# Graph layer on one core: the next batch's preparation spread over three tiles, the last bank of picks reduced by VectorE, and a new order of work on ScalarE

## What is computed

```python
mask = A != 0                                  # A: 8 x 1024 x 1024
vals, idx = top_k(where(mask, -arange(N), -inf), 25)   # the first 25 neighbours of a row
agg = max over those neighbours of X[idx]      # X: 8 x 1024 x 128
agg = where(degree <= 25, maximum(agg, 0), agg)
out = relu(concat([X, agg]) @ W + b)
x = layernorm(X + out)
```

## Time and profile before

| | us |
|---|---|
| median of 3 runs (lowest, highest) | 750.28 (745.78, 757.25) |
| the profiled execution | 752.01 |
| its span in the trace | 750.3 |

### The profile page before, as it was taken

The page is one execution under the profiler, slowest core; times in us unless marked ns, Lnnn a source line. Parts: engine busy times, 40 slices in busy tenths (PEclk is TensorE's granted clock), DMA queues, the critical chain, the costliest instruction groups (busy, mean ns, idle before and its releaser), DMA issues.

```text
span 750.3 us, 13181 instructions
## 1 busy us (share of the span) xinstructions
PE 560.5 (75%) x3836; PEld 321.3 (43%) x3888; DVE 631.5 (84%) x948; ACT 483.2 (64%) x911; POOL 263.3 (35%) x318
## 2 busy tenths in 40 slices
PE   3767876877779677788868777788876977777772
PEld 2444443544335344354435444445443544444331
DVE  5888799977998789889998867989998879987794
ACT  6735675558855578557974757747895569643554
POOL 2525413353034431336313442044513444054400
PEclk9699999999989889799999988999999999999996
DMA  7611220313024120233204312043202411020102
GB/s 240 204 33 63 65 86 16 134 58 109 3 74 141 55 95 11 74 132 92 76 9 130 121 51 72 2 137 116 88 35 75 141 59 44 2 58 26 37 1 58
DMA packets 32682, 56.68 MB, mean 76 GB/s; under 512 B 4515, under 2 KB 21158, under 8 KB 32550
## 3 DMA queue, kind: packets, MB, share of 16 engines
q1 hardware_dynamic: 26150, 42.08, 16.6%
q0 software_dynamic: 6400, 13.12, 6.3%
HBM read 50.99 MB, written 4.19 MB: 74 GB/s over the span
## 4 chain that ended last, share of the span: by engine, by line
PE 29%; DVE 26%; issue 18%; ACT 9%; DVEq 8%; another core or an unknown queue 6%; DMA 4%; SPq 0%; ACTq 0%; POOL 0%; POOLq 0%
PE pair L977 20%; DVE part L714 9%; DVE agg_t L814 5%; DMA adj_sb<-in_adj 4%; DVE hot L708 4%; DVEq L786 2%; PE half L977 2%; DVE g_val L756 2%; ACT maskT L511 2%; DVE g_feat L785 2%; DVEq L826 1%; PE misc L1037 1%; ACT row_work L642 1%; PE p_maskT L949 1%
## 5 line engine op out<-in xcount | busy, mean ns | idle before, releaser
L977 PE MATMUL pair<-hot,x_part 128*128 128x512 bf16 (+2 forms) x1608 | 390.8, 382 | 86.9 <-DVE part L714 49.9
L714 DVE TENSOR_REDUCE part<-pair 128x128 f32<-128x1024 f32 x256 | 311.1, 1218 | 91.0 <-PE pair L977 68.9
L977 PEld LDWEIGHTS pair<-hot,x_part 128*128 128x128 bf16 x1608 | 146.5, 101 | 246.1 <-issue 76.6
L406 POOL DMA_INDIRECT g_feat<-in_x,g_idx x200 | 191.7, 959 | 121.8 <-issue 89.7
L443 POOL TENSOR_TENSOR y_sb<-relu_sb,x_sb 128x128 f32<-128x128 f32 x64 | 30.6, 478 | 342.5 <-ACT relu_sb L570 342.4
L814 DVE TENSOR_REDUCE agg_t<-part 128x128 f32<-128x1024 f32 (+2 forms) x56 | 113.6, 2028 | 0.2 <-ACT part L577 0.2
L511 ACT ACTIVATE maskT<-p_maskT 128x1024 bf16<-128x1024 bf16 x56 | 57.0, 1018 | 60.5 <-PE p_maskT L949 26.9
L708 DVE TENSOR_SCALAR hot<-V 128x1024 bf16<-128x1024 bf16 x224 | 84.5, 390 | 0.0
L577 ACT ACTIVATE part<-half 128x512 f32<-128x512 f32 x56 | 33.4, 597 | 69.6 <-PE half L977 51.2
L502 ACT ACTIVATE mask<-adj_sb 128x1024 bf16<-128x1024 int32 x56 | 58.9, 1053 | 26.3 <-DMA adj_sb<-in_adj 22.8
L518 ACT ACTIVATE V<-p_V 128x512 bf16<-128x512 f32 x98 | 58.3, 595 | 9.5 <-issue 5.0
(11 more groups left out here) (93 smaller groups left out, 590.0 us busy)
## 6 DMA issues: line engine op xcount, KB each, us to landing
adj_sb<-in_adj SPq DMA_DIRECT2D x56, 512.0 KB
g_adj<-in_adj SPq DMA_DIRECT2D x8, 512.0 KB, 4.1
x_sb<-in_x SPq DMA_DIRECT2D x8, 512.0 KB
out<-y_sb SPq DMA_DIRECT2D x7, 512.0 KB
g_feat<-in_x,g_idx POOLq DMA_INDIRECT x200
out<-y_sb SPq DMA_DIRECT2D x1, 448.0 KB
w_sb<-in_W SPq DMA_DIRECT2D x1, 128.0 KB, 7.0
out<-y_sb SPq DMA_DIRECT2D x1, 64.0 KB
```

The source lines that it names most:

```text
L406: pool.indirect_dma_start(out=g_feat[w][:, k, :], out_offset=None, in_=x_rows, in_offset=bass.IndirectOffsetOnAxis(ap=g_idx[w][:, k:k + 1] ...
L714: dve.tensor_reduce(part[:, par(q, s), BANK + p], pairs[buffer_of(s, p)][:, :, :, :].rearrange("f a k i -> f i (a k)"), AX.X, ALU.max).the ...
L977: last = pe.matmul(dst, x_part[:, q, part_no, kb], one_hot, start=(part_no == 0), stop=(part_no == PARTS - 1))
```

## The change

1. **Stagger.** While tile m is picked, TensorE transposes the mask of tile m+8 (`FRONT + 1`) and counts and multiplies for tile m+7 (`FRONT`), and ScalarE makes the mask of tile m+9. Before, the transpose was of tile m+7 and the mask of m+8. `ahead(i, q, s, k)` gives the tile k places on. The prologue makes one mask, one transpose and one copy more than before; on ScalarE the extra mask stands ahead of the first one-hots.
2. **The odd bank.** A tile's groups are three pairs, then the odd bank (`HALF_PLACE = 3`), then the other pairs. VectorE reduces the odd bank like a pair (`reduce_group`, 4 slots to 1); `copy_half` is gone. `part` is now stored with the slots innermost, and `merge` reads 5, 6 or 7 slots that lie side by side.
3. **TensorE's order.** Rank half 0 stands after the transposes, at the first group; the linear layer after the third; rank half 1 after the odd bank. The level is read at the end of the tile, right before the branch. `turn_features` for tile 0 moves to the end of tile 5.
4. **ScalarE's order.** One-hots of ranks 0 and 1 come first in the tile, the mask late, tile 0's relu at the end of the batch. The splits of x move one tile later, GpSimd's two also.
5. **VectorE.** `gathered_max` runs in four parts among the reductions of tile 6, no longer in one piece behind tile 6; it waits for the gathered rows at the second group. Violations are counted after the second group of tile 1, no longer the first, and levels set after the fifth group.
6. SyncE loads the rows of tile m+10 (`FRONT + 3`) at step m and ScalarE uses them at its step m+1 (before: tile m+7, used at ScalarE's step m-1).

The core of the diff (`...` marks what is left out):

```diff
+HALF_PLACE = 3
+FRONT = 7
+def groups(depths):
+    filled = banks(depths)
+    pairs = [[(kb, r, n, BANK * h + place) for h in range(2) for kb, r, n, place in filled[2 * p + h]]
+             for p in range(len(filled) // 2)]
+    return pairs[:HALF_PLACE] + [filled[-1]] + pairs[HALF_PLACE:]
...
-        part = sb("part", [P, 2, BANK + MAX_PAIRS, P], F32)
+        part = sb("part", [P, 2, P, MAX_GROUPS], F32)
...
+        def ahead(i, q, s, k):
+            t = s - 1 + k
+            b = q + t // MT
+            i, q, s = i + b // 2, b % 2, t % MT + 1
+            return None if isinstance(i, int) and 2 * i + q >= B else (i, q, s)
...
-                    if not last:
-                        sp.wait_ge(s_mask, pos(ni, nq, s) - 1)
-                        load_adj(ni, nq, s)
+                    to_load = ahead(i, q, s, FRONT + 3)
+                    if to_load:
+                        sp.wait_ge(s_mask, pos(*to_load) - 1)
+                        load_adj(*to_load)
...
                 if not (isinstance(m, int) and m < 2):
-                    act.wait_ge(s_half, m - 1)
+                    act.wait_ge(s_pair, picked_two_before(i, q, s))
...
-            def copy_half(i, q, s):
...
-                nc.scalar.activation(part[:, par(q, s), 0:BANK], half[:, :, :], ACT.Copy).then_inc(s_halfc, 1)
...
-            def reduce_pair(i, q, s, p):
+            def reduce_group(i, q, s, p):
                 dve.wait_ge(s_pair, pair_no(i, q, s, p) + 1)
-                dve.tensor_reduce(part[:, par(q, s), BANK + p],
-                                  pairs[buffer_of(s, p)][:, :, :, :].rearrange("f a k i -> f i (a k)"),
+                dve.tensor_reduce(part[:, par(q, s), :, p], slots_of(s, p)[:, :, :].rearrange("f k i -> f i k"),
                                   AX.X, ALU.max).then_inc(s_used, 1)
...
-                dve.wait_ge(s_halfc, m + 1)
-                dve.tensor_reduce(agg_t[:, par(q, s)], part[:, par(q, s), 0:BANK + PAIRS[s]].rearrange("f k i -> f i k"), AX.X,
+                dve.tensor_reduce(agg_t[:, par(q, s)], part[:, par(q, s), :, 0:COUNT[s]], AX.X,
                                   ALU.max).then_inc(s_agg, 1)
...
+            GATHERED = {1: (0,), 2: (1,), 3: (2, 3), 4: (4, 5)}
...
-                    if s == 6:
-                        dve.wait_ge(s_g0, 16 * K * (2 * i + q + 1))
-                        gathered_max(0, q, s_agg0)
...
-                pe.wait_ge(s_xtc, m + 1)
                 pe.matmul(p_V[:, :], rank_bf[:, :], maskT[:, par(q, s), h * N // 2:(h + 1) * N // 2],
...
+                elif not (start and p == HALF_PLACE):
+                    pe.wait_ge(s_used, pair_no(i, q, s, p) - since_last_use(s, p) + 1)
```

More of the change, by code:

```diff
@@ L77, in build @@
     LEVELS = 2
-    BANKS = {s: banks(DEPTHS[s]) for s in range(1, NT)}
-    PAIRS = {s: len(BANKS[s]) // 2 for s in range(1, NT)}
-    FIRST = {s: sum(PAIRS[t] for t in range(1, s)) for s in range(1, NT)}
-    BATCH_PAIRS = sum(PAIRS.values())
-    MAX_PAIRS = max(PAIRS.values())
+    GROUPS = {s: groups(DEPTHS[s]) for s in range(1, NT)}
+    COUNT = {s: len(GROUPS[s]) for s in range(1, NT)}
+    FIRST = {s: sum(COUNT[t] for t in range(1, s)) for s in range(1, NT)}
+    BATCH_GROUPS = sum(COUNT.values())
+    MAX_GROUPS = max(COUNT.values())
+    PAIR_FIRST = {s: sum(COUNT[t] - 1 for t in range(1, s)) for s in range(1, NT)}
     RANKS = max(d[0] for d in DEPTHS.values())
-    assert all(sum(piece[2] for piece in bank) == BANK for s in BANKS for bank in BANKS[s])
-    assert all(len(BANKS[s]) % 2 == 1 for s in BANKS) and BATCH_PAIRS % 2 == 0
+    assert FRONT == MT
+    assert all(sum(piece[2] for piece in group) == (BANK if p == HALF_PLACE else 2 * BANK)
+               for s in GROUPS for p, group in enumerate(GROUPS[s]))
+    assert sum(COUNT[s] - 1 for s in COUNT) % 2 == 0
     assert all(d[HIGH_BLOCKS] <= LOW and list(d) == sorted(d, reverse=True) for d in DEPTHS.values())
@@ L174, in build @@
         shift = sb("shift", [P, 2, NT], F32)
-        pairs = [psum(f"pair{i}", [P, 2, 4, P], F32) for i in range(2)]
-        half = psum("half", [P, 4, P], F32)
+        pairs = [psum(f"pair{i}", [P, 2 * BANK, P], F32) for i in range(2)]
+        half = psum("half", [P, BANK, P], F32)
         p_maskT = psum("p_maskT", [P, N], BF16)
@@ L583, in step @@
                     m = pos(i, q, s)
[L584 to L591 removed]
+                    nxt = ahead(i, q, s, 1)
+                    to_rank, to_turn, to_mask = (ahead(i, q, s, FRONT + k) for k in range(3))
+                    if s == 2 and not is_first(i, q):
+                        relu(pi, pq, MT)
+                    if nxt:
+                        first_rank(*nxt)
+                        second_distance(*nxt)
+                    if to_rank:
+                        copy_V(*to_rank, 0)
+                    if to_turn:
+                        copy_maskT(*to_turn)
                     act.wait_ge(s_xt, m + 1)
@@ L800, in redo @@
                 dve.wait_ge(s_fg, m + 1)
-                gathered_max(1, 0, s_fagg)
+                gathered_max(1, 0, s_fagg, range(6))
                 dve.wait_ge(s_ft, m + 1)
-                dve.wait_ge(s_halfc, m + 1)
-                for p in range(BANK + PAIRS[s]):
-                    last = dve.tensor_copy(part[:, par(q, s), p], p_xt)
+                for p in range(COUNT[s]):
+                    last = dve.tensor_copy(part[:, par(q, s), :, p], p_xt)
                 last.then_inc(s_xdone, 1)
@@ L1101, in step @@
                             out_free(i, q, -1)
-                        if not last:
-                            count(ni, nq, s)
+                        if to_rank:
+                            count(*to_rank)
                         if not begin:
```

270 lines of the change are left out of this document (126 added, 144 removed).

## The result

| | us |
|---|---|
| forecast (range) | 688 (664 to 730) |
| changed kernel, median of 4 runs (lowest, highest) | 760.38 (756.95, 761.05) |
| kernel before, median of 4 runs beside it | 749.64 (745.78, 757.25) |
| changed to before, 95% interval | 1.0151 (1.0097 to 1.0206) |
| profiled execution of the changed kernel, its span | 761.05, 759.4 |

The change makes the kernel 1.5% slower; the forecast of 8% faster has the wrong sign. The experiments came in four groups of runs, in which the kernel before took 743.50, 743.36, 694.80 and 693.47 us; so times are compared only inside a group, as ratios to the kernel before there. Executions that fell into a slower state of the chip are left out of these medians, of the ratios and of the times of the experiments. A ratio can differ by up to 0.6% from the quotient of the two medians.

What follows compares the result with a forecast made beforehand. VectorE sets the pace, interrupted by a chain through TensorE and ScalarE. Sum: 28.0 + 1.05 prologue + 577 VectorE work + 65 idle + 15.3 = 686.4 us span, + 1.7 outside = 688 us; range 664 to 730.

Steps and rivals of the forecast that it cites:

- Merge: VectorE's merges, reading slots side by side, cost 825, 958 and 1091 ns; 63 us saved.
- The layout saves less: Rival: merge's slope stays 1.74 ns or strided writes cost, 26 to 28 us back, 714 to 716 us; chance 0.14.
- Odd bank: VectorE's 56 reductions of 512 values from PSUM take 682 ns each, adding 33 us; ScalarE loses 56 copies, 33 us.
- Stagger: TensorE's waits for maskT (28.8 us) and x transposed (13.2), and ScalarE's for adjacency loads (22.8), go.
- the idle time, 65 us: VectorE's idle time in the batches falls to 28 + 37 = 65 us instead of 100; bounds 45 and 100.
- The border: At each change of tiles VectorE idles 0.5 us awaiting TensorE's first pair after its signal: 28 us over 56 tiles.
- Tile 6: Gathered maximum cut into parts no longer than 1.75 us, so TensorE's 3.4 us stand mostly goes.
- The rest, 37 us: VectorE idle from a closed chain through ScalarE and TensorE, plus everything unexplained: 4.6 us a batch, 37 us.
- The waits only move: Rival: TensorE and VectorE have little slack, idle stays near 100 us, half the merge saving, 737 us; chance 0.11.
- ScalarE's circle: Rival: closed chain of ScalarE's copies, mask and one-hots with TensorE's work becomes the bound, 774 us at most; chance 0.07.
- Only the border is left: Rival: all ScalarE waits vanish and clock comes back, idle 28 us at changes of tiles, 651 us; chance 0.08.
- The level read is exposed: Rival: TensorE's level read right before each branch costs it 45 us in all, 733 us; chance 0.09.

Runs made afterwards that it cites:

- the fourth group: Later runs, including the unaltered changed kernel (699.18 us, ratio 1.0093) and the kernel before again (693.60 us), both traced.
- opening the two locks: Changed kernel with TensorE's signal wait only in the extra-levels branch, next tile's one-hots one reduction earlier, gathered maximum behind the branch: 665.60 us, ratio 0.9593.
- the fastest kernel: Same kernel as in opening the two locks: changed kernel with later signal wait, earlier one-hots and maximum behind the branch; 665.60 us, ratio 0.9593.

## Why the prediction was wrong

**What bounds it: right in kind, wrong in one reading.** VectorE sets the pace and is interrupted through TensorE. But I took the named waits for the time that could be won. The counts' 28.8 us for `maskT` came, in part, from standstills of ScalarE that the ordinary order doesn't explain. Timeline of the kernel before:

```profile
150.37 0.61 PE L949 MATMUL p_maskT<-ident_bf,mask 128*128 128x128 bf16 x8
...
151.20 1.04 ACT L532 ACTIVATE x_part<-x_sb 128x1024 bf16<-128x1024 f32 x1
...
155.65 1.02 ACT L511 ACTIVATE maskT<-p_maskT 128x1024 bf16<-128x1024 bf16 x1 [3.40 <-remote]
...
156.82 0.34 PE L971 MATMUL misc<-ones_bf,maskT 128*128 128x1 bf16 x8 [4.06 <-ACT maskT L511]
```

The transposes ended at 150.98, ScalarE was free from 152.24, and yet it began at 155.65. Over the whole trace ScalarE's idle time without a named releaser is 81.3 us, and in the fourth group, with the same kernel and the same durations, 5.0 us; its wait there:

```profile
PE misc L971 <- ACT maskT L511: 5.0, 9, 0.8
```

The change didn't take them away: at groups other than the first VectorE idles 35.1 us before and 54.3 after in the first comparison, and 3.2 and 6.5 in the fourth group, with the same two kernels. What causes them was not found.

**Merge: right.** Estimated 825, 958 and 1091 ns, measured 809, 942 and 1076. "The layout saves less" is refuted, by its reads and by its writes.

**Odd bank: right in duration, wrong in its meaning.** 682 ns estimated, 684 measured. I said that ScalarE's copy "is worth nothing by itself". By the order of the code it was worth its place: as the one group that VectorE didn't reduce, it let VectorE's signal come a bank before TensorE's last work.

**Net on VectorE: about right.** 30 us less forecast; 25.3 in the first comparison, 35.6 in the fourth group, of which about 9 are fewer collisions with GpSimd.

**Prologue: not contradicted.** The first reduction starts at 33.0 us instead of 31.98; 1.05 us were forecast. In the fourth group it is 32.34 and 32.06, so the close match is in part luck.

**Stagger: right in what it removes, small in worth.** The named waits went; alone it gives 1.1%, in a group where little of the 28.8 us stood.

**The failed step is the idle time, 65 us.** Over the whole span VectorE idled 759.4 - 606.2 = 153.2 us; by the forecast it was 686.4 - (631.5 - 30) = 84.9. These 68.3 us, and 4.7 us more work of VectorE, are the 73.0 us by which the span missed 686.4. In front of reductions, for which the 65 us stood, it idled 124.1 us; the remaining 9 us stand elsewhere. The step failed in three places.
- *The border.* "0.5 us x 56 = 28 us, now in every tile." Measured for the first groups without tile 7: 69.8 - 24.4 = 45.4 us, 0.9 us for each of 48. In the fourth group 59.9 - 24.7 = 35.2 us, 0.7 each. I read one undisturbed change, at which only the signal held, and left the one-hots out as a second condition. Nor did I add up the border of the kernel before: it already idled 54.3 us there.
- *Tile 6.* "Its 3.4 us stand of TensorE mostly goes." It grew to 5.8, since the parts of the maximum, the odd bank and the last pair all stand ahead of the signal. I cut the maximum into pieces on paper and didn't ask on which side of the signal the pieces lie. Price: 24.4 us, once a batch 3.05, of which some 1.3 are TensorE's lower clock behind the stand, for which the prediction counted nothing.
- *The rest, 37 us.* 54.3 us. The same kernel has 6.5 in the fourth group, so most of it is not the order of work but the standstills above, whose cause is open.

**Rivals.** *The waits only move* (737 us) was the nearest in kind and too mild: idle time isn't kept, it grows. *ScalarE's circle* had the right sign and the wrong mechanism; making its copies earlier didn't help. *Only the border is left* is nearly the state of the fourth group, where other groups idle 6.5 us, but with a border of 60 us. *The level read is exposed*: the stands in front of first pairs have named causes, and opening the two locks in the fourth group brought the idle time at first groups from 59.9 to 21.9 us, about that of the kernel before (20.8), with the level read left in its place. That leaves no room for 45 us; it was not varied by itself.

**My own test of the sum** (idle 90 us or more means that this step is wrong) gives the verdict: 124.1 us.

## What to carry to other kernels

For each engine that waits at a border, list every condition of its first instruction and what the other engine still has ahead of each signal; work that still stands in front of such a signal holds the other engine, however small its pieces are cut. A group that the pacing engine doesn't reduce can be the cover of the border, so price its place as well as its duration. Wait for a signal at the point where the resource is really used (here in a branch that is rarely taken), and open all conditions together: one of two gave 1 to 2% here, both 5%.

## What the runs showed of the hardware

- A write with a step of 28 bytes costs VectorE's reduction nothing measurable (1218 to 1220 ns; it writes one value for 8 read), and a spaced write costs ScalarE's copy of 512 f32 from PSUM 1083 instead of 597 ns.
- VectorE's step of 768 f32 in SBUF takes 958 ns alone. In six of the eight batches of the changed kernel GpSimd's split of x ran beside it, and it took 1.57 to 2.48 us (1759 ns on average over all eight). In all six it ended 0.81 to 0.82 us after the split did, whenever it had begun. One-hots are hit too: one of 256 values took 1.97 us beside a split in the fastest kernel, where 0.21 is usual.
- The same kernel took 743.36 us in one group of runs and 693.47 in another on the same chip. Its traces at 750.3 and 689.1 us have durations on VectorE and ScalarE that agree (1218 and 1214 ns for a pair). What differs is ScalarE's idle time without a named releaser (81.3 and 5.0 us) and the mean granted clock of TensorE (0.921 and 0.956, busy 560.5 and 539.9 us). Which comes first, and what holds the engines, stays open.
- Behind a stand of 5.79 us six picks took 2.74 instead of 1.46 us, at a granted clock of 0.50 instead of 1.00. In seven of the eight tiles 7 the clock was 0.50 behind stands of 5.79 to 7.12 us, and 0.64 behind the one of 4.43. So each of these stands cost TensorE its own length and up to 1.3 us more.
